# A fused transformer block in 8 tiles: where Wqkv lands, and the order of the first two tiles' work

## What is computed

```python
x = x + matmul(q(LN(x), s1, z1), q(ctx, s2, z2))           # batched, K = 1024
qkv = LN(x) @ Wqkv                                         # 1024 x 1088: 32 query heads of 32, one k, one v
x = x + softmax(causal(q k^T * 32**-0.5 + alibi)) v @ Wo   # Wo 1024 x 1024
h = LN(x); r = softmax(h @ gate_w.T)                       # 8 experts
x = x + (h * (r @ in_scale)) @ sign(weight).T * (r @ out_scale) + bias
```

## Time and profile before

| | |
|---|---|
| Time, median of 3 runs | 471.52 us (471.43 to 472.24) |
| Profiled execution, its own time | 472.27 us |
| its span | 470.5 us |
| TensorE matmuls busy | 384.4 us, 82% |
| VectorE, ACT, GpSimd busy | 306.9, 266.3, 122.8 us |
| Moved by DMA | 90.42 MB, 192 GB/s |
| Mean granted TensorE clock | 0.941 of 2.4 GHz |

### The profile page before, as it was taken

The page is one execution under the profiler, slowest core; times in us unless marked ns, Lnnn a source line. Parts: engine busy times, 40 slices in busy tenths (PEclk is TensorE's granted clock), DMA queues, the critical chain, the costliest instruction groups (busy, mean ns, idle before and its releaser), DMA issues.

```text
span 470.5 us, 9730 instructions
## 1 busy us (share of the span) xinstructions
PE 384.4 (82%) x4000; PEld 261.4 (56%) x4000; DVE 306.9 (65%) x580; ACT 266.3 (57%) x316; POOL 122.8 (26%) x146
## 2 busy tenths in 40 slices
PE   0342936679859999999899989998999899979565
PEld 0102914438625596559565956694669556935342
DVE  4408636698364885878688868777877786295331
ACT  1775495856838566666666655765586551241110
POOL 4201083524111150315031503150324031212202
PEclk9999966689969999999999999999999999999859
DMA  5995998679974765476547654765473001001001
GB/s 205 426 341 202 380 339 326 203 272 372 343 261 136 271 224 182 148 283 208 181 160 277 214 173 181 260 229 176 166 268 137 1 2 46 3 0 47 0 1 45
DMA packets 17122, 90.42 MB, mean 192 GB/s; under 512 B 3440, under 2 KB 3440, under 8 KB 8880
## 3 DMA queue, kind: packets, MB, share of 16 engines
q1 hardware_dynamic: 13408, 81.01, 47.1%
q10 hardware_dynamic: 3664, 8.69, 5.1%
HBM read 85.50 MB, written 4.19 MB: 191 GB/s over the span
## 4 chain that ended last, share of the span: by engine, by line
PE 64%; DVE 14%; ACT 7%; issue 6%; DMA 5%; POOL 2%; ACTq 1%; POOLq 0%; SPq 0%; DVEq 0%
PE R L1289 9%; PE T L1126 7%; PE R L1081 6%; PE R L1083 6%; PE R L1082 6%; PE R L1159 5%; PE R L1161 5%; PE R L1162 5%; ACT b L453 5%; PE C L1107 5%; PE T L1248 3%; DMA ring<-ctx 2%; DVE Pr L848 2%; PE R L1183 2%; DMA ring<-L_attn_Wqkv 1%
## 5 line engine op out<-in xcount | busy, mean ns | idle before, releaser
L453 ACT ACTIVATE b<-ring,quant,qpar 128x2048 uint8<-128x2048 f32 x64 | 132.5, 2092 | 13.0 <-DMA ring<-ctx 10.5
L1159 PE MATMUL R<-T_hi,Wqkv_hi 128*128 128x128 f16 x512 | 89.6, 221 | 0.0
L1161 PE MATMUL R<-T_lo,Wqkv_hi 128*128 128x128 f16 x512 | 89.5, 221 | 0.0
L1162 PE MATMUL R<-T_hi,Wqkv_lo 128*128 128x128 f16 x512 | 89.5, 221 | 0.0
L1107 PE MATMUL C<-b,aT 128*64 128x512 f16 x256 | 40.6, 447 | 17.2 <-ACT b L453 13.4
L1081 PE MATMUL R<-Wo_hi,attT_hi 128*128 128x512 f16 x128 | 49.1, 383 | 5.6 <-DVE Wo_lo L716 5.1
L1159 PEld LDWEIGHTS R<-T_hi,Wqkv_hi 128*128 128x128 f16 x512 | 50.8, 99 | 0.5
L1161 PEld LDWEIGHTS R<-T_lo,Wqkv_hi 128*128 128x128 f16 x512 | 50.7, 99 | 0.2
L1162 PEld LDWEIGHTS R<-T_hi,Wqkv_lo 128*128 128x128 f16 x512 | 50.7, 99 | 0.0
L1289 PE MATMUL R<-sgn,T_hi 128*128 128x512 fp8e4 x128 | 50.6, 396 | 0.0
L1289 PE MATMUL R<-sgn,T_lo 128*128 128x512 fp8e4 x128 | 50.3, 393 | 0.0
(11 more groups left out here) (134 smaller groups left out, 866.3 us busy)
## 6 DMA issues: line engine op xcount, KB each, us to landing
ring<-ctx SPq DMA_DIRECT2D x64, 1024.0 KB, 5.7
ring<-L_attn_Wqkv SPq DMA_DIRECT2D x8, 544.0 KB, 5.2
XN<-x ACTq DMA_DIRECT2D x8, 512.0 KB, 3.6
ring<-L_attn_Wo SPq DMA_DIRECT2D x4, 1024.0 KB, 6.7
ring<-L_ffn_weight SPq DMA_DIRECT2D x4, 1024.0 KB, 4.9
out<-X ACTq DMA_DIRECT2D x8, 512.0 KB, 2.6
alibi_sb<-alibi SPq DMA_DIRECT2D x1, 512.0 KB, 7.1
bias_sb<-L_ffn_bias SPq DMA_DIRECT2D x1, 512.0 KB, 8.1
```

The source lines that it names most:

```text
L453: e.activation(b8[:, c % BRING, :], ring[:, slot, :], ACT.Identity, scale=qR2, bias=qZ2).then_inc(s_rf[slot], 1)
L1159: e.matmul(dst, hi, rows[0], start=k == 0 and g == 0, stop=False, skip_group_check=True)
L1161: e.matmul(dst, hi, rows[1], start=False, stop=False, skip_group_check=True)
L1162: last = e.matmul(dst, lo, rows[0], start=False, stop=k == KT - 1, skip_group_check=True)
```

## The change

Storage and loads. Wqkv's raw pieces land directly in the bytes that later hold Wo (7 pieces) and the signs (1), so they take no ring slot: SP issues all 8 without a wait behind tile 0's context. Wo's first high part waits until all low parts of Wqkv are made. The four scalars go to ACT's queue ahead of `load_x`, the small constants to SP's between context pieces 3 and 4, `alibi` between pieces 3 and 4 of tile 1, `bias` behind `weight`.

Computation. The factor 1024 of LN(x1) moves from `inv_std` into the copies of T1, and `inv_std` has two operations instead of three, in all steps. The f16 copies of the router tables go from ACT to VectorE, step -1, and both tables are built by GpSimd in step -1.

Orders. Steps 0 and 1 have lists of their own on every engine. In step 1, context(1, 3), x1, norm1 and T1 move into the first half. TensorE's second half becomes kv, Ta0, queries 0, Ta1, Tk, queries 1, T0, all four projections, scores, T2, router, inscale, context(2, 0), context(2, 1). From step 2 on the lists are as before.

```diff
+    T_ORDER_1 = [("M", "PT00"), ("M", "PT01"), ("M", "PT10"), ("M", "PT11"), ("F", "T10"), ("F", "T11"),
+                 ("M", "Ta0"), ("M", "Ta1"), ("F", "Tk"), ("N", "T0"), ("M", "T20"), ("M", "T21"),
+                 ("M", "rl"), ("M", "rT"), ("M", "is0"), ("M", "is1")]
+
+    T_ORDER_0 = [("F", "T10"), ("F", "T11"), ("N", "T0"), ("F", "Tk")]
+
+    @classmethod
+    def order(cls, i):
+        return {0: cls.T_ORDER_0, 1: cls.T_ORDER_1}.get(i, cls.T_ORDER)
+
...
-        Wo = [sb(f"Wo_{p}", [P, KT, H], F16) for p in ("hi", "lo")]
+        Wo_hl = sb("Wo", [P, 2, KT, H], F16)
+        Wo = [Wo_hl[:, p] for p in range(2)]
         sgn = sb("sgn", [P, KT, H], FP8)
+        under_wo = Wo_hl[:, :, :, :].rearrange("p a k n -> p (a k n)").bitcast(F32)
+        under_sgn = sgn[:, :, :].rearrange("p k n -> p (k n)").bitcast(F32)
+        wqkv_raw = [under_wo[:, k * NQKV:(k + 1) * NQKV] for k in range(KT - 1)] + [under_sgn[:, 0:NQKV]]
...
         def uses(t, c):
 
-            return t * 2 + c // RING + (0, 2, 4)[min(t, 2)]
+            return t * 2 + c // RING + (2 if t > 1 else 0)
+
+        def weight_uses(kind):
+
+            return uses(1, ITEMS - 1) + {"wo": 1, "ffn": 2}[kind]
+
+        def weight_piece(k):
+
+            return ring[:, k, :].rearrange("p (k n) -> p k n", k=2)
```

SP and GpSimd:

```diff
+            def load_context(t, first, count):
+                for c in range(first, first + count):
+                    pair, b = divmod(c, 2)
+                    src = ctx_v[t * 2 + b:t * 2 + b + 1, :, pair * 2 * H:(pair + 1) * 2 * H]
+                    load_piece(c % RING, uses(t, c), ring[:, c % RING, :],
+                               src.rearrange("o p n -> (o p) n"))
...
             def first_half(s):
                 if not s.front:
                     return
+                load_context(s.i, 0, 4)
+                if s.is_step(0):
+                    load_constants()
                 if s.is_step(1):
+                    e.dma_start(alibi_sb[:, :], alibi).then_inc(s_alibi, 16)
+                load_context(s.i, 4, 4)
+                if s.is_step(0):
+                    for k in range(KT):
+                        e.dma_start(wqkv_raw[k], wqkv_v[:, k, :]).then_inc(s_lw[k], 16)
+                if s.is_step(1):
+                    for k in range(KT // 2):
+                        load_piece(k, weight_uses("wo"), weight_piece(k), wo_v[:, 2 * k:2 * k + 2, :])
+                    for k in range(KT // 2):
+                        load_piece(k, weight_uses("ffn"), weight_piece(k), wt_v[:, 2 * k:2 * k + 2, :])
                     e.dma_start(bias_sb[:, :], bias.rearrange("(o n) -> o n", o=1)
                                 .broadcast_to([P, H])).then_inc(s_bias, 16)
-                for c in range(ITEMS):
-                    pair, b = divmod(c, 2)
-                    src = ctx_v[s.i * 2 + b:s.i * 2 + b + 1, :, pair * 2 * H:(pair + 1) * 2 * H]
-                    load_piece(c % RING, uses(s.i, c), ring[:, c % RING, :],
-                               src.rearrange("o p n -> (o p) n"))
...
-            def inv_std(k, t, factor):
+            def inv_std(k, t):
 
                 e.wait_ge(s_st[k], t + 1)
                 link(e.tensor_tensor(rstd[k][:, 0:1], mv[k][:, 1:2], consts[:, 1:2], ALU.add))
-                link(e.tensor_tensor(rstd[k][:, 1:2], rstd[k][:, 0:1], consts[:, 0:1], ALU.pow))
-                e.tensor_tensor(rstd[k][:, 2:3], rstd[k][:, 1:2], consts[:, factor:factor + 1],
-                                ALU.mult).then_inc(s_rstd[k], 1)
+                e.tensor_tensor(rstd[k][:, 1:2], rstd[k][:, 0:1], consts[:, 0:1], ALU.pow)\
+                    .then_inc(s_rstd[k], 1)
...
                 if s.is_step(1):
-                    prepare_scales(1)
-
+                    inv_std(1, s.i)
...
-                if s.front:
-                    inv_std(1, s.i, 3)
+                if s.front and not s.is_step(1):
+                    inv_std(1, s.i)
                 if s.next:
-                    inv_std(0, s.i + 1, 2)
+                    inv_std(0, s.i + 1)
                 if s.middle:
-                    inv_std(2, s.i - 1, 2)
+                    inv_std(2, s.i - 1)
...
-                if s.is_step(0):
+                if s.is_step(-1):
                     prepare_scales(0)
+                    prepare_scales(1)
```

ACT:

```diff
+            def wqkv_hi(first, count):
+                for k in range(first, first + count):
+                    e.wait_ge(s_lw[k], 16)
+                    e.activation(Wqkv[0][:, k, :], wqkv_raw[k], ACT.Identity, scale=C_W).then_inc(s_whi, 1)
+
+            def wo_hi(k):
+                e.wait_ge(s_ld[k], (weight_uses("wo") + 1) * 16)
+                if k == 0:
+                    e.wait_ge(s_wlo, KT)
+                e.activation(Wo[0][:, 2 * k:2 * k + 2, :], weight_piece(k), ACT.Identity, scale=C_W)\
+                    .then_inc(s_whi, 1)
+
+            def sign(k):
+                e.wait_ge(s_ld[k], (weight_uses("ffn") + 1) * 16)
+                e.activation(sgn[:, 2 * k:2 * k + 2, :], weight_piece(k), ACT.Sign, scale=1.0,
+                             saturate=False).then_inc(s_rf[k], 1)
...
-                        T[:, s.bank(f"T1{c}"), :], 1.0, s_t1hi)
+                        T[:, s.bank(f"T1{c}"), :], C_LN, s_t1hi)
...
+                if s.is_step(0):
+                    e.wait_ge(s_const, SMALL_CONST)
...
+            for n, scalar in enumerate((s1_in, z1_in, s2_in, z2_in)):
+                e.dma_start(quant[:, n:n + 1], scalar.rearrange("(o c) -> o c", o=1).broadcast_to([P, 1]))\
+                    .then_inc(s_quant, 16)
             load_x(Step(-1))
...
+            def entry():
+                s = Step(-1)
+                conv(s.i + 1, 0)
+                conv(s.i + 1, 1)
+                conv(s.i + 1, 2)
+                t0_copy(s)
+                conv(s.i + 1, 3)
+                conv(s.i + 1, 4)
+                conv(s.i + 1, 5)
+
+            def second_half_0(s):
+                load_x(s)
+                conv(s.i, 7)
+                wqkv_hi(0, 3)
+                t1_hi(s, 0)
+                t1_hi(s, 1)
+                wqkv_hi(3, 5)
+                for c in range(4):
+                    conv(s.i + 1, c)
+                kv_copy(s)
+                q_hi(s, 0)
+                q_hi(s, 1)
+                k_hi(s)
+                t0_copy(s)
+                conv(s.i + 1, 4)
+                conv(s.i + 1, 5)
+
+            def second_half_1(s):
+                load_x(s)
+                exp(s, 1, 0)
+                exp(s, 1, 1)
+                pt_hi(s, 1, 0)
+                pt_hi(s, 1, 1)
+                t1_hi(s, 0)
+                t1_hi(s, 1)
+                wo_hi(0)
+                kv_copy(s)
+                ta_hi(s, 0)
+                ta_hi(s, 1)
+                wo_hi(1)
+                wo_hi(2)
+                q_hi(s, 0)
+                k_hi(s)
+                wo_hi(3)
+                q_hi(s, 1)
+                for k in range(4):
+                    sign(k)
+                t0_copy(s)
+                t2_copy(s, 0)
+                t2_copy(s, 1)
+                conv(s.i + 1, 0)
+                router_exp(s)
+                conv(s.i + 1, 1)
+                rt_copy(s)
+                conv(s.i + 1, 2)
+                conv(s.i + 1, 3)
+                xs_hi(s, 0)
+                xs_hi(s, 1)
```

VectorE:

```diff
+            def wqkv_lo(first, count):
+                for k in range(first, first + count):
+                    e.wait_ge(s_whi, k + 1)
+                    lo_part(Wqkv[1][:, k, :], wqkv_raw[k], Wqkv[0][:, k, :], C_W, s_wlo)
+
+            def wo_lo(first, count):
+                for k in range(first, first + count):
+                    e.wait_ge(s_whi, KT + k + 1)
+                    hi, lo = (w[:, 2 * k:2 * k + 2, :] for w in Wo)
+                    lo_part(lo, weight_piece(k), hi, C_W, s_rf[k])
+
+            def prepare_scales():
+
+                e.wait_ge(s_const, SMALL_CONST)
+                e.tensor_copy(insc[:, :], in_raw).then_inc(s_prepa, 1)
+                e.tensor_copy(outsc[:, :], out_raw).then_inc(s_prepa, 1)
...
                     row_max(s.i - 1, 1, 1)
+                if s.is_step(1):
+                    x1(s)
                 if m:
                     pt_lo(s, 0, 0)
                     pt_lo(s, 0, 1)
                 if b:
                     result(s, 0)
+                if s.is_step(1):
+                    norm1(s)
                 if m:
                     attn_rows(s, 0, 0)
                     attn_rows(s, 0, 1)
-                if m:
                     pt_lo(s, 1, 0)
                     pt_lo(s, 1, 1)
                 if b:
                     result(s, 1)
-                if m:
+                if s.is_step(1):
+                    t1_lo(s, 0)
+                    t1_lo(s, 1)
+                elif m:
                     ta_lo(s, 0)
+                if m:
                     attn_rows(s, 1, 0)
                     attn_rows(s, 1, 1)
...
+            def entry(s):
+                stats0(s)
```

(143 more changed lines are left out.)

155 lines of the change are left out of this document (51 added, 104 removed).

## The result

The changed kernel takes 482.36 us (median of 4 runs, 481.06 to 485.08), the kernel before in the same session 471.88. The ratio is 1.0229, 95% interval 1.0181 to 1.0276: slower, though the interval leaves open whether by more than 2%. Forecast were 478.0 us and the range 469.5 to 485. The profiled execution took 481.89, its span is 480.1.

What follows compares the result with a forecast made beforehand. TensorE bounds from step 2 on, so only the stretch before 135.96 counted: context(2, 2) 6.4 us later, less 0.3 at the end, sum +6.1 on the profiled 472.27 or median 471.52; forecast 478.0 us, range 469.5 to 485.

Steps and rivals of the forecast that it cites:

- The wait of T0: Step 1, second half: T0 waits for VectorE's norm0; TensorE stands for 12.5 us with 48 projection matmuls behind it.
- the order behind it: Step 1: projections follow T0, 10.3 us plus 2 for half clock, ending at T + 31.8.
- Entry: Start of the kernel: scalars ahead of X on ACT's queue make the activations 1.0 us later, bounds 0 to 3.5.
- rival (B): Scalars share DMA engines with the context; entry 3.5 us late instead of 1, on top of half clock: 484; chance 0.15.
- GpSimd: Step -1: both scale tables built by GpSimd end at 38.2, a new wait of 1.2 us before the inverse deviation.
- the contention: Step -1: VectorE's two casts beside GpSimd's X add cost one or the other up to 1.9 us through the shared port.
- Step 0: First Wqkv product at 43.6, context(1, 0) at 59.8, scores at 61.8 or 63.7: a gain of 8 to 10 us.
- Clock: Step 1 to the first query half's end: 87.3 at full clock, 94.8 at half from 60 on; middle taken, 91.
- the full-clock column: Step 1 times with full clock throughout: scores at 61.8, first half of the queries ending at 87.3.
- x1 as a new wait: Step 1, first half: x1 takes VectorE 3.1 us ahead of PT00's and PT01's low parts, so the attention waits.
- The tail: End of step 1: 5.3 us from x2 to T2's copy, then 14.2 with six ACT conversions before context(2, 2).

Runs made afterwards that it cites:

- run 3: Changed kernel with the four scalars' loads back at the head of SP's queue, ahead of the context: 476.84 us, ratio 1.0143.
- run 5: Changed kernel with SP issuing nothing until the scalars land: 478.04 us. Its first view shows the unaltered changed kernel, 3 to 15 us.
- Run 4: Changed kernel with GpSimd's second router table moved from step -1 to step 1's first half, behind the inverse deviation: 481.45 us, ratio 1.0226.
- run 8: Changed kernel with T0 last, scalars on SP, second table late, x1 late and tile 2's conversions woven between copies: 464.22 us, ratio 0.984.
- run 1: The changed kernel once more, unaltered, as the measure for its neighbours: 482.92 us, ratio 1.0277.
- run 7: Changed kernel with x1 of tile 1 behind the low parts of PT00 and PT01 on VectorE: 483.04 us, ratio 1.0238.
- run 6: Changed kernel with ACT converting the first six pieces of tile 2 ahead of T2's copies: 476.99 us, ratio 1.0101.
- runs 2: Changed kernel with T0 of step 1 moved behind the four projections on TensorE, nothing else: 470.14 us, ratio 0.9986.
- run 9: Changed kernel with T0 of step 1 behind the projections and the scalars back at the head of SP's queue: 465.04 us, ratio 0.9876.
- run 10: Changed kernel with T0 behind the projections, scalars back on SP and tile 2's six conversions ahead of T2's copies: 471.25 us, ratio 1.0016.
- 11: Changed kernel with T0 behind the projections, scalars on SP, six conversions early and the second table late: 472.88 us, ratio 1.0042.
- 12: The version with all edits (464.22 us), with norm2 ahead of norm0 and T2's transposes and router ahead of T0: 466.29 us, ratio 0.9898.

## Why the prediction was right, and where its sum was off

**The wait of T0** was read rightly: 12.5 forecast, 12.76 in seven profiles. So was the order behind it. The stations, in us (T is the end of the first query half; run 3 has the scalars back on SP's queue):

```
station                     forecast     after        run 3
first Wqkv product            43.6       49.06        43.48
scores, full / half clock   61.8 / 63.7  66.7 (full)  61.1 (full)
T                             91         93.95        88.28
T0 starts                  T + 18.8      T + 18.84    T + 18.83
projections end            T + 31.8      T + 32.2     T + 32.1
context(2, 2) starts       T + 51.3      T + 51.67    T + 51.64
```

From T on the sum is right to 0.4 us. Up to T it is not: two terms are off, in opposite directions.

**Entry** is the term that was mis-sized: 1.0 with bounds 0 to 3.5; measured were 6.2 (18.03 less 11.86). I took the scalars' own time as given, let them land at 8.84 as before, and asked only what they do to X. But the scalars themselves became late: they landed at 15.0. They had been first in time, now they run beside the context. The prediction's rival (B) had the reason right and its size at little more than half. The Trainium skill, DMA: Bandwidth & Descriptors, section on queues, rings and completion order, has each DMA engine take its queue rows in turn by packets. I concluded from that that the scalars would not wait. The traces do not contradict the rule but my use of it. That section's packet is a group of descriptors, which need not be what the profile counts as one. In the 12 us of run 5's first view SP's queue moved 634 of the profile's packets and ACT's 646, about one for one, but 3.92 MB against 0.36. With such turns the 512 packets of four bytes have to let about as many of 8 KB pass, and the queue with the big packets has the greater part of the time.

**GpSimd**: tables that end at 38.2 and a wait of 1.2 were forecast. They ended at 43.7, 2.3 us behind the statistics that VectorE had ready at 41.43; norm1 waited for them. Run 4 shows that wait to be worth 2.2 up to the first product. The two casts beside the X add show the contention that the prediction priced at up to 1.9; from the X add to the tables' end it took 19.1 us instead of 18.5, so that it cost 0.6. VectorE:

```profile
24.43 0.67 DVE L800 CAST insc<-X 32x1024 f16<-32x1024 f32 x1
25.03 2.38 DVE L801 CAST outsc<-ln2T 32x1024 f16<-32x1024 f32 x1
```

The second cast took 2.38 beside the X add, the first 0.67. The X add took 2.26 instead of 1.90. The Trainium skill, SBUF — State Buffer, section on who interferes with whom, names an exclusive lock on a shared port pair. By that rule one of two such instructions stands until the other is done. The trace agrees, in this cast, which ended 0.55 behind the X add, and in norm1 of run 8, 2.60 instead of 0.81.

**Step 0**: a gain of 8 to 10 us at the scores was forecast; it was 4.8 (66.7 against 71.5), since the first product came 5.5 late. In run 3 it was 10.4 (61.1).

**Clock**: the contexts and scores of step 1 ran at full clock; I had taken the middle of full and half. By the full-clock column T would be 87.3 + 5.5 = 92.8; it was 93.95. So T is only 2.95 off: the middle stood 3.7 above the full-clock column, 2.6 of which was not needed, and that hid about half of the entry's 5.5. This was luck. Run 3, without the late scalars, has T at 88.28, 2.7 under the 91, and run 1, the same kernel as here, has it at 95.41: the row of its stretch from 84.4 to 88 gives a granted clock of 0.50 (T1's transposes took 1.94, here 1.25). **x1 as a new wait** was there (the pv products waited 3.75 us for a low part), but run 7 shows that to put x1 back gains nothing.

**The tail** came out as forecast (5.4 for 5.3, 14.0 for 14.2), and the conversions in it cost 4 to 6 by run 6.

What was expected of the change as a whole, a front that gains and a wait that takes it back, is shown by runs 2, 3 and 9: -12.8 for the wait, -6.1 for the entry, 465.0 with both, which is 5.9 under the kernel before. Not settled: why the clock in step 1 was at full this time and in some other profiles lower (step 1's router took 1.92 in the changed kernel's profile and 3.56 in that of run 6, with a granted clock of 0.50), and the true worth of the table's place. Nor does any run take back the new place of Wqkv or the order of step 0 alone: that these are what puts run 9 under the kernel before is argued from the stations, not shown.

## What to carry to other kernels

An instruction that waits blocks everything behind it on its engine: before an operation with a far producer is put into an order written by hand, follow the producer's own queue up to it, and put ready work ahead. Here one line moved gave 10 to 13 us back. A place that is right in one order is wrong in the next: the same six conversions gained 5.9 us behind a late T0 and lost 6.2 behind an early one. Small loads on which the first instruction waits should be issued before any large transfer on any queue, not only ahead on their own.

## What the runs showed of the hardware

- Loads of a few bytes to 128 partitions: 12.86 us to landing beside running 1 MB loads on another queue (changed kernel), 6.7 at the head of the queue of those loads (run 3), 4.3 with those loads held back (run 5); the slowest of four in each case.
- Context pieces of 1 MB, once requested back to back, were converted every 2.45 us (113.30, 115.76, 118.21 in run 10: 2.10 of conversion and 0.35 of waiting for the load), so that there ScalarE was bound by the loads and not by its 2.1.
- Norm1 of one tile took 0.81 us alone, and 2.46 to 2.60 where GpSimd had begun a table's product 0.06 to 0.21 us before (runs 4, 8, 11 and 12).
